# Two gated layers on one core: the low parts of the first expert weights made by GpSimd from rows that ScalarE scales in full

## The reference, cut to what matters

```python
x = x + tanh(g_xattn[0]) * einsum(quant_act(layernorm(x)), quant_weight(ctx))   # first phase: FP8 product
x = x + tanh(g_ffn[0])   * ternary_linear(rms_norm(layernorm(x)), W0)           # W0 rounded to -1, 0, 1
x = x + tanh(g_xattn[1]) * attention(layernorm(x), ctx, ctx)
x = x + tanh(g_ffn[1])   * mixture(layernorm(x), router_w, Wa, Wb)              # 8 experts of rank 128, top 2
```

## Time and profile before

| | us |
|---|---|
| three runs | 1982.36, 1982.72, 1984.06 |
| their median | 1982.72 |
| the profiled execution, its own time | 1985.46 |
| span of the profiled execution | 1983.7 |
| busy in the span: PE, DVE, ACT, POOL | 1851.1, 1559.9, 1264.0, 846.4 |
| mean granted TensorE clock | 0.986 of 2.4 GHz |

### The profile page before, as it was taken

The page is one execution under the profiler, slowest core; times in us unless marked ns, Lnnn a source line. Parts: engine busy times, 40 slices in busy tenths (PEclk is TensorE's granted clock), DMA queues, the critical chain, the costliest instruction groups (busy, mean ns, idle before and its releaser), DMA issues.

```text
span 1983.7 us, 26460 instructions
## 1 busy us (share of the span) xinstructions
PE 1851.1 (93%) x8968; PEld 838.5 (42%) x8968; DVE 1559.9 (79%) x2386; ACT 1264.0 (64%) x2045; POOL 846.4 (43%) x1100
## 2 busy tenths in 40 slices
PE   1699999996699999999999999999999999999998
PEld 0244444442244444444444444444444444444443
DVE  8899999888877777777777777777777777777662
ACT  4798999675656665666665665656656665666650
POOL 3555565333344443444444443443444444444420
PEclk9999999998799999999999999999999999999998
DMA  9587777797888888878888888888888888888772
GB/s 210 160 207 201 225 199 189 190 210 221 159 151 170 169 178 170 168 154 166 170 163 174 165 171 169 170 174 169 160 162 169 164 170 167 165 172 168 152 143 54
DMA packets 923975, 340.50 MB, mean 172 GB/s; under 512 B 849728, under 2 KB 898880, under 8 KB 923840
## 3 DMA queue, kind: packets, MB, share of 16 engines
q1 hardware_dynamic: 923840, 338.81, 80.9%
HBM read 93.36 MB, written 33.55 MB: 64 GB/s over the span
## 4 chain that ended last, share of the span: by engine, by line
PE 73%; issue 4%; DVE 2%; POOL 2%; DMA 1%; ACT 1%; SPq 0%; POOLq 0%; DVEq 0%
PE sc L1080 16%; PE accs L1060 11%; PE accs L1062 11%; PE accs L1061 11%; PE accs L1101 6%; PE accs L1118 6%; PE accs L1102 6%; PE accs L1103 6%; POOL slot L599 1%; DMA slot<-slot 1%; POOL slot L592 1%; PE accs L1129 0%; DMA wb_lo<-in_L_ffn_Wa 0%; DVE tiny L1585 0%; PE accs L1131 0%
## 5 line engine op out<-in xcount | busy, mean ns | idle before, releaser
L1590 DVE SCALAR_TENSOR_TENSOR slot<-arena,tiny,slot 128x1024 f16<-128x1024 f32 x256 | 346.4, 1353 | 169.1 <-ACT slot L885 165.6
L885 ACT ACTIVATE slot<-arena,tiny 128x1024 f16<-128x1024 f32 x256 | 290.9, 1145 | 251.8 <-POOL tiny L710 247.0
L1080 PE MATMUL sc<-arena,slot 128*128 128x512 f16 x1536 | 375.8, 383 | 19.7 <-ACT arena L872 17.3
L708 POOL TENSOR_SCALAR tiny<-tiny 128x1 f32<-128x1 f32 x256 | 117.4, 459 | 519.1 <-ACT arena L872 519.1
L1585 DVE TENSOR_REDUCE tiny<-sc 128x1 f32<-128x1024 f32 x256 | 311.7, 1218 | 20.0 <-PE sc L1080 20.0
L872 ACT ACTIVATE arena<-sc,tiny,head_tab 128x1024 f32<-128x1024 f32 x256 | 308.4, 1205 | 8.6
L1080 PEld LDWEIGHTS sc<-arena,slot 128*128 128x128 f16 x1536 | 147.9, 98 | 211.8 <-ACT arena L872 32.2
L710 POOL TENSOR_TENSOR tiny<-tiny,neg_one 128x1 f32<-128x1 f32 x256 | 224.7, 878 | 21.3
L1101 PE MATMUL accs<-probs,arena 128*128 128x512 f16 x512 | 196.1, 383 | 12.3 <-issue 10.8
L864 ACT ACTIVATE tiny<-tiny,head_tab 128x1 f32<-128x1 f32 x256 | 74.3, 290 | 207.3 <-DVE tiny L1585 207.3
L1060 PE MATMUL accs<-wb_hi,slot 128*128 128x512 f16 x512 | 194.1, 379 | 2.7 <-DMA slot<-slot 2.7
(11 more groups left out here) (214 smaller groups left out, 2907.3 us busy)
## 6 DMA issues: line engine op xcount, KB each, us to landing
arena<-in_x SPq DMA_DIRECT2D x32, 512.0 KB, 4.0
x_scratch<-arena SPq DMA_DIRECT2D x32, 512.0 KB, 3.7
slot<-x_scratch SPq DMA_DIRECT2D x32, 512.0 KB, 3.3
slot<-in_ctx SPq DMA_DIRECT2D x32, 512.0 KB, 4.2
out<-arena SPq DMA_DIRECT2D x31, 512.0 KB, 3.6
slot<-in_L_ffn_Wa SPq DMA_DIRECT2D x12, 512.0 KB, 4.5
slot<-in_L_ffn_Wb SPq DMA_DIRECT2D x9, 512.0 KB, 5.2
wb_hi<-in_ctx SPq DMA_DIRECT2D x64, 64.0 KB, 2.3
```

Source lines behind the costliest of these rows:

```text
L885: act.activation(high, full, ACT.Identity, scale=rinv[c % 4][:]).then_inc(s_ph.sem, 1)
L1080: mm = pe.matmul(sc[:, c % 2, h * HALF:(h + 1) * HALF], q[i][:, c * P:(c + 1) * P], k[j][:, h * HALF:(h + 1) * HALF], start=start, stop=stop)
L1590: dve.scalar_tensor_tensor(out=low, in0=full, scalar=rinv[c % 4][:], in1=high, op0=ALU.mult, op1=ALU.subtract).then_inc(s_pl.sem, 1)
```

## The change

`weight_low` leaves VectorE's list and enters GpSimd's, in the same step, behind `x_round` and `x_low`. It is now a plain subtraction (a TENSOR_TENSOR) that needs its first operand already scaled. So ScalarE's `weight_high` writes the scaled rows of Wa back to the raw buffer in float32, waits for its own write, and then casts them into the high part: three instructions where there were two. The waits of `load_prep` on `wa_lo_set` are unchanged, but another engine raises it. The values are the same but for rounding.

```diff
--- before.py
+++ after.py
@@ -253,7 +253,7 @@
         wf_root = signal("wf_root")
         wp_in, w_n, w_clip, w_tern, w_turned = (signals("wp_in", 2, 32), signal("w_n"), signal("w_clip"), signal("w_tern"),
                                                 signal("w_turned", 16))
-        wa_hi_set, wa_lo_set = signal("wa_hi_set"), signal("wa_lo_set")
+        wa_full, wa_hi_set, wa_lo_set = signal("wa_full"), signal("wa_hi_set"), signal("wa_lo_set")
         wb_in, wb_hi_set, wb_lo_set = signals("wb_in", KB, 16), signal("wb_hi_set"), signal("wb_lo_set")
         g_pool, g_dve, g_pe, go = signal("g_pool"), signal("g_dve"), signal("g_pe"), signal("go")
 
@@ -640,6 +640,10 @@
                 pool.tensor_scalar(ocol[:], wab[:], gate[:, 3:4], 1.0 / (AMP ** 3 * HID_SHRINK), ALU.mult,
                                    ALU.mult).then_inc(wf_pool.sem, 1)
 
+            def weight_low(r):
+                pool.wait_ge(wa_hi_set.sem, wa_hi_set.at(r))
+                pool.tensor_tensor(wa_lo[:, r, :], raw(1, r), wa_hi[:, r, :], ALU.subtract).then_inc(wa_lo_set.sem, 1)
+
             for n in range(X_EARLY):
                 x_rstd(n)
             for n in range(X_EARLY):
@@ -654,6 +658,8 @@
                 if is_x(j + 2) and j + 2 >= X_EARLY:
                     x_round(j + 2)
                     x_low(j + 2)
+                if PREP < j <= PREP + KB:
+                    weight_low(j - PREP - 1)
                 if j == -4:
                     pool.wait_ge(gates.sem, 1)
                     c_tables(0)
@@ -801,7 +807,9 @@
             def weight_high(r):
                 act.wait_ge(wp_in[r % 2].sem, wp_in[r % 2].at(r // 2))
                 act.activation(raw(0, r), raw(0, r), ACT.Identity, scale=winv[:]).then_inc(w_n.sem, 1)
-                act.activation(wa_hi[:, r, :], raw(1, r), ACT.Identity, scale=wamp[:, 0:1]).then_inc(wa_hi_set.sem, 1)
+                act.activation(raw(1, r), raw(1, r), ACT.Identity, scale=wamp[:, 0:1]).then_inc(wa_full.sem, 1)
+                act.wait_ge(wa_full.sem, wa_full.at(r))
+                act.copy(wa_hi[:, r, :], raw(1, r)).then_inc(wa_hi_set.sem, 1)
 
             def key_high(n):
                 act.wait_ge(kx_in.sem, kx_in.at(n))
@@ -1410,11 +1418,6 @@
                 dve.wait_ge(w_clip.sem, w_clip.at(r))
                 after(dve, w_turned, r - 1)
                 dve.tensor_scalar(W0T, w, ROUND_INT, ROUND_INT, ALU.add, ALU.subtract).then_inc(w_tern.sem, 1)
-
-            def weight_low(r):
-                dve.wait_ge(wa_hi_set.sem, wa_hi_set.at(r))
-                dve.scalar_tensor_tensor(out=wa_lo[:, r, :], in0=raw(1, r), scalar=wamp[:, 0:1], in1=wa_hi[:, r, :],
-                                         op0=ALU.mult, op1=ALU.subtract).then_inc(wa_lo_set.sem, 1)
 
             def output_low(r):
                 dve.wait_ge(wb_hi_set.sem, wb_hi_set.at(r))
@@ -1492,7 +1495,6 @@
                     x_split(j + 2, 2)
                 if PREP < j <= PREP + KB:
                     ternary_round(j - PREP - 1)
-                    weight_low(j - PREP - 1)
                 if next_x and j >= PREP:
                     round_x(j + 2)
                 if is_x(j + 4) and j + 4 >= X_EARLY:
```

## The result

The changed kernel takes 1991.58 us, the median of six runs (1987.54 to 1993.65), against 1982.70 us for six runs of the kernel before. The two medians differ by 8.9 us. The ratio of the two series is 1.0040, with a 95% interval of 1.0027 to 1.0054, which is 7.9 us with 5.4 to 10.7 in the interval: the change makes the kernel slower, by 0.4%. The forecast was 1991.0, in a range of 1987.0 to 1996.0. In some series of the experiments one or two executions took 3300 to 10400 us; the ratios leave them out.

What follows compares the result with a forecast made beforehand. In steps 24 to 32 a ring through ScalarE's weight instructions was taken to bound the kernel. Ring delay of 4.3 us, late loads and final ScalarE work accumulated to 8.3: 1982.72 + 8.3 = 1991.0 us, range 1987.0 to 1996.0.

Steps and rivals of the forecast that it cites:

- The ring: Steps 24 to 32: cycle from centre to centre through ScalarE's weight instructions, 1.07 us longer in four turns, 4.3 us late.
- VectorE's saving: Eight instructions of 1.28 us fewer on VectorE: worth nothing in the ring, counting once at the stage's end.
- step 5: Stage's end: ScalarE's work on piece 7, then x1_square(30); x1_max(30) waits for it, finish_x1(31) starts 8.3 us late.
- The queue: SyncE's weight loads wait for GpSimd's subtraction, 7.0 us after the statistics, 4.1 us late; x's transposes wait behind them.
- The landing: Time from issue of W0's load until the pair of pieces has arrived: 0.42 + 5.5 = 5.9 us.
- step 3: Piece 6 and tile 31's transposes land at 450.9 us; product(31) waits for them and ends 7.0 us late.
- TensorE's gaps: New gaps before products 30 and 31, as a sign of the forecast.
- rival B: Everything late: landings of 7.1 us cost 3.6 us more, TensorE's clock may fall; 13 us slower, 1995.7 us, chance 0.12.
- A: Loads land in 0.42 + 4.3 us, leaving mainly the cast in the ring: 5.1 us slower, 1987.8 us, chance 0.18.
- the port's 1.6: VectorE's x_safe also waits for GpSimd's subtraction, so x_scale slips 0.4 us in each of four turns.
- C: VectorE closes the ring, so 1.2 us less in each of eight steps gives 9.6 us: 1973.1 us, chance 0.05.
- D: No difference: cast falls in ScalarE's idle 3.97 us, queue's delay is absorbed before product(31); 1983.7 us, chance 0.08.

Runs made afterwards that it cites:

- e1: The changed kernel with the subtraction back on VectorE in its old place, ScalarE's three weight instructions kept: 1987.78 us, ratio 1.0013, stage 98.43 us.
- e4: The kernel before with ScalarE's weight_high moved ahead of centre and GpSimd's x_round ahead of x_rstd: 1980.17 us, ratio 0.9967, stage 87.06 us.
- e8: The kernel before with only weight_high moved ahead of centre, GpSimd's order unchanged: 1983.28 us, ratio 0.9997, stage 93.74 us.
- e2: The changed kernel with ScalarE's two weight instructions as before, GpSimd's subtraction kept (low parts wrong in value): 1987.00 us, ratio 1.0015, stage 97.60 us.
- e3: The changed kernel with GpSimd's subtraction at the head of its step, ahead of x_rstd and x_round: 1988.08 us, ratio 1.0017, stage 99.44 us.
- e5: The changed kernel run once more, beside a second series of the kernel before: 1990.66 us, ratio 1.0034, stage 101.84 us.
- e6: The changed kernel with weight_high ahead of centre, x_round ahead of x_rstd, and the subtraction one step earlier: 1982.02 us, ratio 0.9991, stage 92.02 us.
- e7: The kernel before, unchanged, as a control: 1984.33 us, ratio 1.0004, stage 93.63 us.

## Why the prediction was right

The time of each event in the stage, in us from the start of x_high(25). "Predicted" is the prediction's time less 363.41:

| | before | predicted | changed |
|---|---|---|---|
| ScalarE starts on piece 4 | 56.78 | 63.8 | 63.27 |
| x_high(30) | 61.47 | 67.0 | 66.45 |
| piece 5 | 69.19 | 75.8 | 75.35 |
| x_high(31) | 72.10 | 78.9 | 78.52 |
| piece 6 | 79.69 | 87.5 | 87.15 |
| product(31) starts | 82.7 | 89.7 | 89.10 |
| piece 7 | 88.85 | 96.5 | 96.33 |
| finish_x1(31) | 93.70 | 102.0 | 101.92 |

- **The ring.** 14.07 us per turn were forecast, 14.09 measured, and the 3.97 us of idle time before centre stayed. The mask waited 1.50 us, where 0.9 to 1.3 were named as the sign. e1 isolates the cast; e4 and e8 show the other way round that the weight instructions were inside, for turns fall when they leave.
- **VectorE's saving is worth nothing.** In the ring so it was: e1 has the saving taken back and the same turn. At the end of the stage x1_max(30) waits for the square, as step 5 said, but the saving doesn't count there either: from the start on piece 7 to finish_x1(31) it is 5.59 us in the changed kernel and 5.59 in e1, where VectorE makes the subtraction.
- **The queue.** The loads leave with the end of GpSimd's subtraction, 6.9 to 7.0 us behind the statistics. e2 shows this part alone (3.9 us, where its expectation said 3.8), e3 takes 2.5 of it away.
- **The landing.** This term was sized too long. It was taken as 5.9 us from the issue of W0; pieces 4, 5 and 6 were there after 5.34, 5.46 and 5.44. This is why the lines of the table up to product(31) came 0.35 to 0.6 us earlier than predicted. That the last line came only 0.1 earlier is in part luck, because an omission runs the other way: step 3 left out that VectorE and GpSimd stop each other at piece 5. VectorE's two rounding instructions took 2.29 and 2.50 us. The first of them met x_low in the kernel before too:

```profile
435.70 2.30 DVE L1409 TENSOR_SCALAR wb_lo<-wb_lo 128x1024 f32<-128x1024 f32 x1
```

  The 2.50 is new (0.69 before). The load of piece 6 waits for the first of GpSimd's two subtractions, which took 2.58 instead of 2.13, and so left some 0.45 us later than it would have. What is left of the difference is in three terms of 0.1 us each, in the queue, in the landing of piece 7 and in ScalarE's work on it. The two subtractions:

```profile
448.63 2.58 POOL L645 TENSOR_TENSOR wa_both<-slot,wa_both 128x1024 f16<-128x1024 f32 x1
451.17 2.57 POOL L645 TENSOR_TENSOR wa_both<-wb_lo,wa_both 128x1024 f16<-128x1024 f32 x1
```

- **TensorE's gaps.** Forecast before products 30 and 31; they are there, of 0.30 and 1.13 us, and 0.86 and 1.04 in e5. A third was not forecast. The transposes of tile 29 stand behind the late loads of piece 4, and in e5 TensorE waits for them:

```profile
433.26 10.52 PE L1027 MATMUL sc<-probs,slot 128*128 128x512 f16 x48 [1.95 <-DMA slot<-slot]
```

  In the first trace of the changed kernel this gap doesn't show, for there the slow product 28 lasted into it. The 1.5 to 3.5 us of rival B are those of the ring (3.56).
- **The rivals.** A, the cast alone, needed loads that land in 4.7 us, and they took 5.3 to 5.5. Its time is what e1 and e3 measure (98.43 and 99.44, against 98.8 by its 5.1 us), where the loads leave early. B needed landings of 7.1 us for pieces 4 to 6, and its loss by the port was not seen in either trace; its sum of 13 also leaves out most of the port's 1.6 that it names, with which it would be 14.5. C falls with e1 and e6, where VectorE's load was varied and never paid. D falls with the turn of 14.09: the cast did not go into the idle 3.97 us.

The agreement of the changed kernel's median with the forecast, 0.6 us, is closer than the measurement, and so partly luck: by their ratios the two series give 7.9 and 6.7 us, by their medians 8.9 and 6.3. The stage is the firmer number. It was 93.70 and 93.63 before, 101.92 and 101.84 after.

## What to carry to other kernels

Before moving an instruction to an idle engine, ask two things of the rows: does the work that must be added to make the move possible stand in a ring, and what does the moved instruction release. Here a plain subtraction needed its operand scaled, which put 1.09 us into a ring four times, and it was the last to free a buffer, so a queue of loads and transposes stood 4 us longer for it. And look at the idle time inside a ring first: moving two instructions of ScalarE into a gap of 3.97 us, and one of GpSimd ahead of a wait, gave 6.6 us in the stage with no arithmetic changed. The first of the two moves alone shortened the turn by 0.25 us and the stage not at all (e8). Then follow the stage to its end: what comes last there, here the landing of the last piece, decides how much of a shorter ring arrives.

## What the runs showed of the hardware that was not expected

- The stop between VectorE and GpSimd is not one of small instructions in particular. In the rows of the changed kernel x_recip, one source, ran its usual 0.21 us at 397.29, in the middle of GpSimd's subtraction (397.12 to 399.24); the next instruction, with two sources in SBUF, took 1.85, until the subtraction had ended. The Trainium skill states this distinction in "SBUF — State Buffer", section "Who interferes with whom": a VectorE instruction with at most one SBUF input, outside the two-port modes, doesn't contend with GpSimd, and one with two contends with a GpSimd instruction that reads SBUF. The trace agrees for these two. Of x_safe, which has one source and is stopped too (1.01 us, 0.23 otherwise), no row shows whether it ran in a two-port mode. Large instructions stop as well, and both sides lose: 2.50 us instead of 0.69 for VectorE's rounding at 449.26, 2.58 instead of 2.13 for GpSimd's subtraction at 448.63.
- The clock. The prediction took the slow product of the earlier trace rows to follow from the gap of 2.48 us before it. It doesn't follow each time. In the same trace the gap of 2.48 us at 413.76 was followed by a product of 10.52, and in e7, the same kernel, so were all three gaps of 2.48 and 2.49 us. Over the ten traces, three of eleven gaps of 2.16 to 2.49 us were followed by a slow product, and eight of nine of 2.98 to 3.57 us; the granted clock was 0.60 from 387.76 to 392.00 in the kernel before, and 0.50 from 423.13 to 428.00 in the changed one. A slow product took up to 1.7 us longer (12.21 for 10.52). None of these decided the time of the stage, which followed the landing of piece 7 in every trace.
- Outside the stage two executions of one kernel differ by microseconds. The stage began at 363.41 and 365.98 in two traces of the kernel before, and the time after it was 1526.6 and 1522.3 us. In those of the changed kernel it began at 369.52 and 367.17, and 1520.1 and 1523.5 us followed. Why is open; no edit here touches these parts. One profile of each kernel, compared by the spans, gives 7.9 us, but by luck: of the changed kernel's the stage began 6.1 us later, and 6.4 us less followed it.
